# Twenty-two attention projections instead of four made ahead of the first expert block, stored as f32 and finished during the expert blocks

## The chip, the cores and the metric

The program runs on one core of one Trainium2 chip. The metric is the device time of one execution in microseconds (us). The kernel before has a median of 1081.95 us over three runs, which lie between 1077.45 and 1082.16 us.

## What is computed

Input x is (4, 1024, 256): 4 sequences ("batches") of 1024 tokens. The reference, cut to what matters:

```python
xn = layernorm(x)
# attention: 8 query heads of 128, one shared key/value head
q = (xn @ Wq + bq), split into 8 heads;  k, v = split(xn @ Wkv + bkv)
q, k = q + pe, k + pe                     # sinusoidal positions
attn = softmax(causal(q @ k.T / sqrt(128))) @ v
s = concat(attn) @ Wo
# mixture of experts: 8 experts, top 2 per token, hidden size 1024
g = silu(sum over top-2 of gate * (relu(xn @ w1[e] + b1[e]) @ w2[e] + b2[e]))
out = x + s * g
```

A "projection" below is one K, Q or V piece: 512 tokens of one batch against 128 columns of a weight, so K, V and each head's Q have two pieces (j = 0, 1) each. Values are kept as pairs of f16 (high and low part), and a product is three f16 matmul passes (`PASSES`), so a K or Q projection is 6 matmuls of 128x512 and a V projection 24 of 128x128.

## The kernel before, in words

Every engine has its own instruction list, written by hand; engines meet through semaphores. There are three stages, one after the other on TensorE.

**Routing (`routing`).** The rows are normalised and turned into `xT`/`xTb_next`; TensorE makes the router's logits (`logits`), then `project(r)` for four projections of batch 0 (K and the first head's Q), `counts()`, and `place(s)` eight times, which waits for VectorE's one-hot tables (`one_hots`) and yields the list of rows for each expert block. ScalarE scales the first two experts' weights (`weights(q)`), VectorE makes their low halves (`first_low(q)`), GpSimd gathers the rows (`gather`), SyncE's queue writes them to DRAM (`keep`) or turns them (`straight`).

**Expert blocks (`experts`).** 40 blocks; block n multiplies up (L933) while block n-1 multiplies down (L942). The first 22 are of 256 rows, then wide (256) and narrow (128) blocks alternate, then the list ends narrow. ScalarE does the relu of a block in four pairs (L1008), then issues in its own list the turned loads of block n+3 (`load`, L218) and the store of y of block n-2 (`store`, L996). VectorE splits the relu into high and low (`split`, L1032 and L1034) and writes y of block n-2 (`rows`, L1044). GpSimd meanwhile alternates `gather(n)` with `split(p)` of the later experts' weights (L261, L263, L265); SyncE alternates `keep(n)` with `stage(p)`, the load of the raw weights into `wstage`. In four of the last ten blocks one of the stored projections is loaded (L919), gets its positions (L1061), is rounded (L1014) and its low half made (L1065).

**Attention (`attention`).** 32 heads (n = 8 x batch + head), each in five groups of score rows (i = 0 to 4, k = 5n + i). TensorE: `scores` (L1242, L1245), `values` of the head before (L1265, L1267), one projection of the table `Jobs` where it has one for k (L1201), and from head 9 on one `o_tile` of 24 matmuls (L1281). VectorE: row maxima (L1426), low half of the probabilities (L1462), and for a projection `job_positions` (L1435) and `job_low` (L1449, for V L1444). ScalarE: exponentials (L1346), high half (L1376), `job_high` (L1366, for V L1361), and one tanh (L1395) per head. SyncE turns the probabilities by DMA (L1571, `b_pT<-b_ph`). `Jobs` puts the two Q pieces of head n+2 at i = 0 and 2 of head n; the K and V pieces of the next batch at i = 1 of heads 4 to 7 of each batch but the last, in a score bank ("S"); and in head 0 and 1 also V of batch 0.

Of the kernel before, what the change touches and what calls it, by code (L numbers as in the profile page):

```python
# [23 lines left out]
C_ID, C_MASK, C_UP, C_E = 0, P, 2 * P, 3 * P  # L24

# [44 lines left out]
def build(nc, x, wq, bq, wkv, bkv, wo, rw, rb, w1, b1, w2, b2, cst, pe, out):  # L70
# [32 lines left out]
    xT_d = nc.dram_tensor("xn_turned", (NB_ - 1, P, QT * 2 * DC * P), F16, kind="Internal").ap()  # L103
    kq_d = nc.dram_tensor("first_kq", (P, 4, 512), F32, kind="Internal").ap()
    wo_d = nc.dram_tensor("wo_split", (P, 2, HEADS, D), F16, kind="Internal").ap()

    def tensors(ctx):
# [31 lines left out]
    kq_t = Arena(nc, moe.at).take("kq_t", [P, 512], F32)  # L139
# [9 lines left out]
    half = Arena(nc, x_at + NT * D * 2)  # L149
    w_raw.append(half.take("a_w_raw1", [P, PIECES, 512], F32))  # L150
    assert half.at <= raw_end
    xTb_next = top.take("xTb_next", [P, QT, 2 * DC, P], F16)
    wq_late = top.take("wq_late", [P, 2 * DC * HEADS * HD], F16)
# [14 lines left out]
    pe_, kqs_, kql_, kqt_, kqa_, kqb_ = (whole.enter_context(nc.semaphore(s)) for s in (  # L168
        "positions_in", "kq_stored", "kq_loaded", "kq_positions", "kq_hi", "kq_lo"))
# [134 lines left out]
class Jobs:  # L304


    def __init__(self, heads):
        self.at, self.order, self.bank = {}, [], []
        for k in range(5 * heads):
            n, i = k // 5, k % 5  # L310
            b = n // HEADS
            job, bank = None, "J"
            if n == 0:
                job = (("Q", 1, 0), ("Q", 1, 1), ("V", 0, 0), ("V", 0, 1), ("Q", 2, 0))[i]
                bank = ("J", "O0", "O1", "J", "O0")[i]
            elif n == 1 and i < 3:
                job, bank = ("Q", 2 + (i + 1) // 2, (i + 1) % 2), "JSJ"[i]
            elif i in (0, 2) and n + 2 < heads:
                job = ("Q", n + 2, i // 2)
            elif i == 1 and n % HEADS >= 4 and HEADS * (b + 1) < heads:  # L320
                job, bank = ("KKVV"[n % HEADS - 4], b + 1, n % 2), "S"
            if job:
                self.at[k] = len(self.order)
                self.order.append(job)
                self.bank.append(bank)
# [4 lines left out]

    def turned(self, q):

        return sum(1 for p in range(q + 1) if self.order[p][0] != "V")
# [10 lines left out]
def routing(v, ctx, sem, psU):  # L344
# [5 lines left out]
    kq_d, kqs_, wq, wkv, wkv_p, pe_ = (v[k] for k in ("kq_d", "kqs_", "wq", "wkv", "wkv_p", "pe_"))  # L350
# [21 lines left out]
    assert dead.at <= v["x_at"] + NT * D * 2  # L372
    spent = Arena(v["nc"], area.at - (NT - QT) * 2 * DC * P * 2 - NT * 2 * D * 2)
    kq_f = spent.take("a_kq_f", [P, 4, 512], F32)
# [41 lines left out]
    turn_bank, psX, psJ = flat[:4], flat[4], flat[5]  # L416
    psL = psX[:, 0:NT * E]
# [12 lines left out]
    s_kw, s_ks, s_kp, s_kc = map(sem, ("kq_weights_in", "kq_weights_split", "kq_projected", "kq_copied"))  # L430
# [23 lines left out]
    def on_tensor(eng):  # L454
# [27 lines left out]
        def project(r):  # L482

            eng.wait_ge(s_ks, 6)
            j, k = r % 2, 0
            for a, b in PASSES:
                for c in range(DC):
                    w = wkv_p[:, a, c, 0:HD] if r < 2 else wq_p[:, a, c, :]
                    mm = eng.matmul(flat[r].rearrange("p (t n) -> p t n", n=P), w, xTb_next[:, 4 * j:4 * j + 4, 2 * b + c, :],
                                    start=(k == 0), stop=(k == 3 * DC - 1))  # L490
                    k += 1
            mm.then_inc(s_kp, 1)
# [37 lines left out]
        for r in range(3):  # L530
# [3 lines left out]
        project(3)  # L534
        for s in range(CHUNKS):
            place(s)
        eng.wait_ge(s_kc, 4)

    def on_scalar(eng):
# [17 lines left out]
        def weights(q):  # L557
            eng.wait_ge(s_w[q // 4], 16)
            eng.activation(halves(q)[0], v["raw_of"](q), ACT.Copy, scale=WS).then_inc(wh0_, 1)

# [35 lines left out]
        for q in range(PIECES):  # L596
            weights(q)
        eng.wait_ge(s_diff, 1)
        eng.activation(ex[:, 0, :], ex[:, 2, :], ACT.Exp).then_inc(s_e, 1)
        for q in range(PIECES, 2 * PIECES):  # L600
# [1034 lines left out]
```

## Time and profile before

| | |
|---|---|
| three timed runs, median | 1081.95 us |
| lowest and highest | 1077.45, 1082.16 us |
| profiled execution, span of its instructions | 1078.8 us |
| mean granted TensorE clock | 0.984 |
| TensorE (PE) busy | 990.9 us, 92% |
| VectorE (DVE) busy | 857.8 us, 80% |
| ScalarE (ACT) busy | 641.9 us, 59% |
| GpSimd (POOL) busy | 336.8 us, 31% |

The page gives no time of the profiled execution apart from its span, 3.15 us below the median and within the three runs. "Busy" is the time in which an engine had an instruction running. In the trace, a time in us counts from the span's start; "[x <-ENGINE tile]" behind a row is how long the engine was idle before it and what ended that. Expert blocks fill 85 to 471 us, attention the rest.

### The profile page before, as it was taken

To read this page: it belongs to the slowest core of one execution; us is meant where nothing else is said; L and a number is where in the kernel's file an instruction comes from. 1 tells how busy PE (TensorE), PEld (TensorE's weight loads), DVE (VectorE), ACT (ScalarE), POOL (GpSimd) and SP (SyncE) were. 2 spreads that over 40 slices of the span, in tenths; PEclk is the share of its full clock that TensorE was granted. 3 is DMA by queue.
4 is the path that set the end of the run, shared out by engine and by line. 5 is a ranking of instruction groups with operands and counts; after the bars stand their busy time and mean duration, and the time that the engine had idled before them with its cause. 6 is when DMAs were issued, how large, how long until landed. Compare 5 with 4: busy or idle time off the path is not lost.

```text
span 1078.8 us, 25081 instructions
## 1 busy us (share of the span) xinstructions
PE 990.9 (92%) x8686; PEld 778.5 (72%) x8686; DVE 857.8 (80%) x1535; ACT 641.9 (59%) x1358; POOL 336.8 (31%) x350
## 2 busy tenths in 40 slices
PE   0747999999999999998989889999999999999997
PEld 0536888888888898865656667767777677677776
DVE  6985776666766455569999999998999999999971
ACT  2722333233333333357888888878888878788860
POOL 3215999989995000020101002121212111112111
PEclk9968999999999999999999999999999999999999
DMA  8778666666666322149887879798999878888992
GB/s 273 211 287 182 157 181 177 174 179 184 171 172 147 95 60 65 46 121 159 171 154 141 157 142 186 152 164 150 172 189 178 150 150 162 153 171 160 181 179 95
DMA packets 410137, 172.58 MB, mean 160 GB/s; under 512 B 351994, under 2 KB 399940, under 8 KB 409252
## 3 DMA queue, kind: packets, MB, share of 16 engines
q1 hardware_dynamic: 352816, 129.80, 57.5%
q10 hardware_dynamic: 50724, 23.50, 8.6%
q0 software_dynamic: 6480, 17.70, 6.5%
q8 instruction: 77, 1.26, 0.5%
q14 instruction: 40, 0.33, 0.1%
HBM read 52.84 MB, written 31.72 MB: 78 GB/s over the span
## 4 chain that ended last, share of the span: by engine, by line
PE 37%; DVE 10%; DMA 5%; ACT 2%; issue 1%; SPq 0%; ACTq 0%; DVEq 0%
PE b_psO L1265 11%; PE b_psS L1242 11%; PE b_psJ L1281 5%; DMA b_pT<-b_ph 5%; PE b_psJ L1201 5%; DVE b_nmax L1426 3%; DVE b_ph L1462 3%; PE b_psS L1292 2%; PE b_psO L1267 1%; PE b_psS L1201 1%; DVE b_outs L1468 1%; ACT b_pr L1346 1%; ACT b_ph L1376 1%; PE b_psS L1245 1%; DVE b_Q L1449 1%
## 5 line engine op out<-in xcount | busy, mean ns | idle before, releaser
L933 PE MATMUL psU<-bxT,w_p 128*128 128x256 f16 (+1 forms) x1920 | 287.5, 262 | 13.3 <-DVE w_p L276 9.3
L1008 ACT ACTIVATE h<-psU,bias 128x256 f32<-128x256 f32 (+1 forms) x320 | 125.3, 448 | 273.6 <-PE psU L933 171.5
L942 PE MATMUL psY<-w_p,hp 128*128 x1704 | 273.4, 273 | 2.1 <-DVE hp L1034 2.1
L1242 PE MATMUL b_psS<-b_kp,b_Q 128*128 128x512 f16 (+3 forms) x1152 | 218.8, 326 | 1.5 <-PEq L1086 1.5
L1346 ACT ACTIVATE b_pr<-b_psS,b_nmax 128x1024 f32<-128x1024 f32 (+7 forms) x256 | 187.0, 735 | 47.9 <-DVE b_nmax L1426 27.1
L933 PEld LDWEIGHTS psU<-bxT,w_p 128*128 x1920 | 188.4, 98 | 34.0 <-issue 15.1
L1265 PE MATMUL b_psO<-b_pT,b_vp 128*128 128x256 f16 x1536 | 189.7, 274 | 20.3 <-issue 13.5
L1462 DVE SCALAR_TENSOR_TENSOR b_ph<-b_pr,b_rrec,b_ph 128x1024 f16<-128x1024 f32 (+7 forms) x256 | 199.4, 810 | 0.0
L1376 ACT ACTIVATE b_ph<-b_pr,b_rrec 128x1024 f16<-128x1024 f32 (+7 forms) x256 | 187.0, 768 | 15.4 <-DVE b_rrec L1455 14.1
L1032 DVE CAST hp<-h 128x512 f16<-128x512 f32 (+1 forms) x160 | 88.9, 556 | 133.7 <-ACT h L1008 127.5
L1426 DVE TENSOR_REDUCE b_nmax<-b_psS 128x1 f32<-128x1024 f32 (+7 forms) x256 | 183.1, 746 | 13.9 <-PE b_psS L1245 12.4
L942 PEld LDWEIGHTS psY<-w_p,hp 128*128 128x128 f16 x1704 | 166.1, 98 | 23.4 <-issue 3.5
L1265 PEld LDWEIGHTS b_psO<-b_pT,b_vp 128*128 128x128 f16 x1536 | 145.0, 98 | 44.1 <-issue 19.1
L1242 PEld LDWEIGHTS b_psS<-b_kp,b_Q 128*128 128x128 f16 x1152 | 103.2, 98 | 78.9 <-issue 2.2
L1539 POOL DMA_INDIRECT b_yg<-expert_outputs,pos x64 | 68.4, 1069 | 246.1 <-DMA expert_outputs<-y 119.5
L1545 POOL TENSOR_TENSOR b_x_row<-b_G,b_x_row 128x256 f32<-128x256 f32 x24 | 17.4, 727 | 368.6 <-DVE b_G L1489 359.8
L1034 DVE TENSOR_TENSOR hp<-h,hp 128x512 f16<-128x512 f32 (+1 forms) x160 | 127.1, 794 | 5.5
L179 POOL DMA_INDIRECT rowx<-xn_split,who x71 | 78.0, 1099 | 65.9 <-DVE who L796 43.4
L1281 PE MATMUL b_psJ<-b_wo,b_outs 128*128 128x256 f16 x576 | 66.9, 273 | 0.0
L265 POOL TENSOR_TENSOR w_p<-wstage,w_p 128x512 f16<-128x512 f32 x48 | 64.5, 1343 | 4.1
L1366 ACT ACTIVATE b_Q<-b_psJ,bias 128x512 f16<-128x512 f32 x59 | 40.6, 687 | 32.5 <-DVE b_psJ L1435 32.1
L1281 PEld LDWEIGHTS b_psJ<-b_wo,b_outs 128*128 128x128 f16 x576 | 55.2, 98 | 6.5
(187 smaller groups left out, 1027.1 us busy)
## 6 DMA issues: line engine op xcount, KB each, us to landing
wstage<-in_L_ffn_w SPq DMA_DIRECT2D x48, 256.0 KB
expert_rows<-rowx SPq DMA_DIRECT2D x67, 128.0 KB
expert_outputs<-y ACTq DMA_DIRECT2D x31, 256.0 KB
a_x_all<-in_L_attn_x SPq DMA_DIRECT2D x8, 512.0 KB, 9.7
a_w_raw<-in_L_ffn_w SPq DMA_DIRECT2D x4, 1024.0 KB, 9.4
xn_split<-a_xp SPq DMA_DIRECT2D x4, 1024.0 KB, 8.9
xn_turned<-a_xT SPq DMA_DIRECT2D x3, 1024.0 KB, 13.7
b_x_row<-in_L_attn_x SPq DMA_DIRECT2D x24, 128.0 KB, 2.5
```

The costliest lines, as they stand in the source:

```text
L933: mm = eng.matmul(psU[w % U][:, g % 2, 0:tiles * P].rearrange("p (t r) -> p t r", t=tiles), weight(n, a * W1 + c * H + g * P, P), bxT[n % ...
L942: mm = eng.matmul(psY[n % 2][:, t, :], hp[n % 2][:, a, g, t * P:(t + 1) * P], weight(n, 2 * W1 + (2 * g + b) * D, D), start=(g == 0 and k ...
L1008: a = eng.activation(h32[w % 4][:, g, 0:rows], psU[w % U][:, g, 0:rows], ACT.Relu, bias=bias[:, ds(e * HT + 2 * q + g, 1)], scale=1.0 / WS)
L1032: eng.tensor_copy(hi, full).then_inc(hh_, 1)
L1034: eng.tensor_tensor(lo, full, hi, ALU.subtract).then_inc(hl_, 1)
L1242: mm = eng.matmul(dst, Q[n % 3][:, a, u * P:(u + 1) * P], kb[:, c, lo:lo + w], start=(kk == 0), stop=(kk == 2 and not last))
L1265: eng.matmul(both, vb[:, a, j, :], pT[:, at:at + hop + 1:hop, :], start=(j == 0 and kk == 0), stop=False)
L1281: mm = eng.matmul(psJ[:, 0:D], outs[b % many][:, a, h, t * P:(t + 1) * P], wo_p[:, e, h, :], start=(h == 0 and kk == 0), stop=(h == HEADS ...
L1346: a = eng.activation(pr[k % 3][:, o:o + w], psS[BUF[i]][:, :, :].rearrange("p a n -> p (a n)")[:, o:o + w], ACT.Exp, bias=nmax[:, at:at + ...
L1376: a = eng.activation(ph[k % 4][:, 2 * o:2 * o + w], pr[k % 3][:, o:o + w], ACT.Copy, scale=rrec[:, at:at + 1])
L1426: a = eng.tensor_reduce(nmax[:, at:at + 1], psS[BUF[i]][:, :, :].rearrange("p a n -> p (a n)")[:, o:o + w], AX.X, ALU.max, negate=True)
L1462: a = eng.scalar_tensor_tensor(ph[k % 4][:, 2 * o + w:2 * o + 2 * w], pr[k % 3][:, o:o + w], rrec[:, at:at + 1], ph[k % 4][:, 2 * o:2 * o ...
```

## The change

A table `FRONT` names 22 projections: K, Q (head 0) and V of batch 0; K and V of batches 1, 2 and 3; Q of heads 8 and 16. Routing makes all of them, from `xTb_next` and `xT`, in six banks in turn (a seventh waits until the first is copied); ScalarE copies each to f32 in SBUF (`copied`), with the weights of expert 1 scaled in between. `gates()` moves behind `first_low` of expert 0. The raw weights of expert 1 go where `xp` was, so their load now waits for `xn_split`. `xTb_next` is written to DRAM too, by a store that waits in SyncE's list for all 22 copies and stands ahead of `keep(4)`; the load of `b2b` then waits until all turned rows have landed. SyncE stores the f32 results, 512 KB at a time, between `keep(n)` and `stage(p)` (11 times).

One projection is finished per wide block from block 6 on (22 blocks): ScalarE loads it (`kq_load`) behind block n-1, VectorE adds positions (not for V), ScalarE rounds it (`kq_high`), VectorE makes the low half in block n+1, and ScalarE stores both halves (`kq_store`). The first `kq_load` waits for all eleven f32 stores. At the end SyncE loads K and Q of head 0 and `xTb_next` back. In attention SyncE loads V of batch 0 at the start, the next batch's K in head 3 and V in head 4 of each batch, and Q of heads 8 and 16 two heads ahead. `Jobs` keeps only Q pieces.

```diff
+FRONT = tuple([(kind, 0, j) for kind in "KQV" for j in (0, 1)] + [(kind, b, j) for b in (1, 2, 3) for kind in "KV" for j in (0, 1)]
+              + [("Q", m, j) for m in (HEADS, 2 * HEADS) for j in (0, 1)])
...
-            if n == 0:
-                job = (("Q", 1, 0), ("Q", 1, 1), ("V", 0, 0), ("V", 0, 1), ("Q", 2, 0))[i]
-                bank = ("J", "O0", "O1", "J", "O0")[i]
-            elif n == 1 and i < 3:
-                job, bank = ("Q", 2 + (i + 1) // 2, (i + 1) % 2), "JSJ"[i]
-            elif i in (0, 2) and n + 2 < heads:
+            if n == 0 and i < 4:
+                job, bank = ("Q", 1 + i // 2, i % 2), ("J", "O0", "O1", "J")[i]
+            elif n and i in (0, 2) and n + 2 < heads and n + 2 not in FRONT_Q:
                 job = ("Q", n + 2, i // 2)
-            elif i == 1 and n % HEADS >= 4 and HEADS * (b + 1) < heads:
-                job, bank = ("KKVV"[n % HEADS - 4], b + 1, n % 2), "S"
...
+        def copied(r):
+            eng.wait_ge(s_kp, r + 1)
+            eng.activation(kq_f[r // 8][:, r % 8, :], job_bank[(r + 2) % 6], ACT.Copy,
+                           scale=1.0 / WS if FRONT[r][0] == "V" else SC / WS).then_inc(kqc_, 1)
...
+    wide = [n for n in range(6, NBLK) if v["ORDER"][n] < TWIN]
+    KQ_AT = {n: r for r, n in enumerate(wide[:JOBS])}
...
+        eng.wait_ge(kqc_, JOBS)
+        eng.dma_start(v["xT_d"][0], v["xTb_next"][:, :, :, :].rearrange("p t h n -> p (t h n)")).then_inc(xk_, 16)
         for n in range(4, AHEAD):
             v["keep"](eng, n)
+        eng.wait_ge(xk_, 64)
...
+            if n - AHEAD - 4 < JOBS // 2:
+                job_store(n - AHEAD - 4)
...
+        def kq_load(r):
+            if r == 0:
+                eng.wait_ge(kqs_[0], 8 * (JOBS - 16))
+                eng.wait_ge(kqs_[1], 8 * 16)
+                eng.wait_ge(xk_, 64)
+            if r >= 2:
+                eng.wait_ge(kqb_, r - 1)
+            eng.dma_start(kq_t[r % 2][:, :], kq_d[:, r, :]).then_inc(kql_[r % 2], 16)
...
+            if n + 1 in KQ_AT:
+                kq_load(KQ_AT[n + 1])
+            if n - 1 in KQ_AT:
+                kq_store(KQ_AT[n - 1])
             if n >= 2:
                 store(n - 2)
```

TensorE before, from the last logits to the first expert block (`a_oh_r` and `a_oh_q` are the one-hot tables of `place`):

```order
L476 MATMUL psU<-a_rw_p,a_xT 128x8 x48
L489 MATMUL psU<-xTb_next,wkv_p 128x512 x12
L489 MATMUL psU<-xTb_next,a_wq_p 128x512 x6
L499 MATMUL psU<-a_one_100,a_M_109 128x128 x2
L504 MATMUL psU<-a_tri_92,a_tot_93 128x264 x2
L505 MATMUL psU<-a_M_109,a_up_99 128x256
L489 MATMUL psU<-xTb_next,a_wq_p 128x512 x6
L511 MATMUL psU<-a_oh_q,a_oh_r 128x71 x64
L885 TENSOR_LOAD blk_e
```

The same place after, without five of the eight `place` steps:

```order
L508 MATMUL psU<-xTb_next,wkv_p 128x512 x12
L508 MATMUL psY<-xTb_next,a_wq_p 128x512 x12
L519 MATMUL psU<-a_one_105,a_M_114 128x128 x2
...
L499 MATMUL psY<-wkv_p,a_xT 128x128 x48
L531 MATMUL psU<-a_oh_q,a_oh_r 128x71 x8
L508 MATMUL psU<-a_xT,wkv_p 128x512 x3
...
L499 MATMUL psU<-wkv_p,a_xT 128x128 x12
L508 MATMUL psY<-a_xT,wkv_p 128x512 x12
L499 MATMUL psU<-wkv_p,a_xT 128x128 x48
L508 MATMUL psU<-a_xT,a_wq_p 128x512 x12
L508 MATMUL psY<-a_xT,a_wq_p 128x512 x12
L934 TENSOR_LOAD blk_e
```

One whole projection more stands ahead of `counts`, six stand between it and the first `place`, half a one stands behind each `place`, and eight behind the last.

ScalarE after, behind the last relu of block 5 and up to the first relu of block 7 (the four `ISA` and six of the eight relus of block 6 left out); before, the rows of lines L1067 and L1077 are absent here:

```order
L226 DMA_TRANSPOSE bxT_69<-expert_rows 128x4x128 [waits x_kept1]
L1067 DMA kq_t_78<-projected 128x512 [waits xT_kept,projected_stored,projected_stored_late]
L1058 DMA expert_outputs<-y_71 128x2x256 [waits e_rows]
...
L1093 ACTIVATE h_3_137<-psU,bias 128x256
L1077 ACTIVATE kq_h_80<-kq_t_78,bias 128x512 [waits kq_positions]
L226 DMA_TRANSPOSE bxT_67<-expert_rows 128x4x128 [waits x_kept2,e_up]
L226 DMA_TRANSPOSE bxT_67<-expert_rows 128x4x128 [waits x_kept3]
L1067 DMA kq_t_79<-projected 128x512
L1058 DMA expert_outputs<-y_72 128x2x256 [waits e_rows]
```

The load of the first projection, with its wait for every f32 store, now stands ahead of the relus of block 6 on ScalarE.

## Rows read from the trace of the kernel before

**Rows 1.** The page: busy tenths of TensorE in 40 slices of 27 us.
```profile
PE   0747999999999999998989889999999999999997
```
**Rows 2.** Windows: busy us (instructions) of each engine, clock, DMA share, GB/s.
```profile
63.00:76.00 13.00, 10.08 (x64) 7.76 (x64) 11.37 (x26) 3.83 (x8) 0.00 (x0) 0.50 0.75 314
76.00:85.00 9.00, 0.00 (x0) 0.00 (x0) 8.83 (x21) 0.00 (x0) 5.79 (x6) 0.50 0.38 100
...
150.00:330.00 180.00, 180.00 (x1660) 161.45 (x1659) 121.35 (x156) 57.57 (x138) 161.80 (x169) 1.00 0.65 177
```
**Rows 3.** Windows again, in attention, cut at the tanh of heads (L1395).
```profile
521.13:538.25 17.12, 15.18 (x119) 10.36 (x118) 16.23 (x30) 14.64 (x32) 1.89 (x2) 1.00 0.88 170
538.25:610.01 71.76, 64.63 (x524) 44.70 (x523) 68.86 (x123) 60.71 (x127) 7.58 (x8) 1.00 0.81 149
663.21:680.62 17.41, 17.41 (x142) 12.60 (x140) 16.68 (x31) 14.86 (x32) 2.98 (x3) 1.00 0.94 183
680.62:756.93 76.31, 76.31 (x628) 54.68 (x625) 70.29 (x127) 61.81 (x127) 11.78 (x12) 1.00 0.85 154
826.21:902.74 76.53, 76.19 (x627) 54.70 (x625) 70.29 (x127) 61.81 (x126) 11.78 (x12) 1.00 0.84 153
```
**Rows 4.** Timeline of PE, routing to first expert block: start us, us, instructions.
```profile
47.97 4.06 PE L489 MATMUL psU<-xTb_next,wkv_p 128*128 128x512 f16 x12
...
55.42 1.46 PE L489 MATMUL psU<-xTb_next,a_wq_p 128*128 128x512 f16 x6
...
64.35 1.26 PE L511 MATMUL psU<-a_oh_q,a_oh_r 128*128 128x71 f16 x8 [7.47 <-DVE a_oh_q L758]
...
85.12 7.55 PE L933 MATMUL psU<-bxT,w_p 128*128 128x256 f16 x54 [9.34 <-DVE w_p L276]
92.51 0.82 PE L942 MATMUL psY<-w_p,hp 128*128 x6
```
**Rows 5.** Timeline of ACT, ahead of the relus of block 1.
```profile
103.32 1.20 ACT L1008 ACTIVATE h<-psU,bias 128x256 f32<-128x256 f32 x3 [8.17 <-DMA expert_rows<-rowx]
```
**Rows 6.** Timelines of SP and ACT behind the last relu of block 5.
```profile
148.91 0.33 SPq L184 DMA_DIRECT2D expert_rows<-rowx  x1
...
148.73 0.47 ACT L1008 ACTIVATE h<-psU,bias 128x256 f32<-128x256 f32 x1
...
151.13 0.60 ACTq L996 DMA_DIRECT2D expert_outputs<-y  x1
152.47 0.84 ACT L1008 ACTIVATE h<-psU,bias 128x256 f32<-128x256 f32 x2 [3.28 <-issue]
```
**Rows 7.** Landing times of a 256 KB load, and of the 1 MB f32 store.
```profile
DMA to landing us min/median/max: 2.9/3.0/3.6
...
first_kq<-a_kq_f ACTq DMA_DIRECT2D x1, 1024.0 KB, 8.2
```
**Rows 8.** Groups by line on DVE, 150 to 330 and 350 to 440 us, then its timeline.
```profile
L1034 DVE TENSOR_TENSOR hp<-h,hp 128x512 f16<-128x512 f32 x70 | 67.3, 961 | 2.4
...
L1061 DVE TENSOR_TENSOR kq_t<-kq_t,pe_sb 128x512 f32<-128x512 f32 x3 | 2.1, 684 | 0.0
...
144.05 1.53 DVE L1034 TENSOR_TENSOR hp<-h,hp 128x512 f16<-128x512 f32 x1
...
150.41 1.02 DVE L1034 TENSOR_TENSOR hp<-h,hp 128x512 f16<-128x512 f32 x1
...
440.98 0.69 DVE L1034 TENSOR_TENSOR hp<-h,hp 128x512 f16<-128x512 f32 x1
```
**Rows 9.** A group by line and form in attention, 640 to 850 us.
```profile
L1449 DVE SCALAR_TENSOR_TENSOR b_Q<-b_psJ,bias,b_Q 128x512 f16<-128x512 f32 x23 | 17.1, 742 | 0.0
```
**Rows 10.** The chain that ended last, heads 0 to 2: start us, us.
```profile
483.11 0.60 DVE b_vp L1444
...
493.83 1.29 PE b_psS L1201 x6
...
516.84 5.62 DMA b_pT<-b_ph
```

## What the change does to the time, predicted

> **What bounds the kernel now.** I read the page first for where TensorE is full, then windows by stage, then the timelines at the places that the change touches. In the slices TensorE is at 8 or 9 tenths nearly everywhere; after the loads of the input the low ones are the third and fourth, at the end of routing [rows 1]. The windows say what that gap is: from 76 to 85 us TensorE executes nothing, from 63 to 76 us only the 64 short `place` matmuls, and its granted clock is 0.50, the 1.2 GHz level, after the 7.47 us without work before the first `place` [rows 2, 4]. The reader is to see there that VectorE is busy for 11.37 of 13 us and 8.83 of 9 us: routing ends with VectorE, and TensorE waits for it. In the expert blocks it is the reverse: 180.00 us busy of 180, VectorE 121.35, ScalarE 57.57 [rows 2]. In attention there are two regimes [rows 3]. From head 9 on TensorE is busy in all of a head's 17.41 us, and the four heads that carry K and V jobs take 76.31 and 76.53 us. In the first heads TensorE has 2 us of holes in 17.12 and VectorE is busy 16.23; the chain that ended last runs there through VectorE and the turned probabilities (5.62 us for one transfer) [rows 3, 10]. So a projection taken out of attention is worth its TensorE time from head 9 on, and less than that before. A projection put into routing is free as far as it lies under VectorE's work.
>
> **Attention: what is taken out.** Eighteen projections leave (12 of K and V, 2 V of batch 0, 4 Q). Cutting at the tanh of each head:
> - Heads 12 to 15 and 20 to 23: they take 76.31 + 76.53 us and would take 8 x 17.41 = 139.28 without a K or V job, as head 11 does [rows 3]: 13.6 us. Their VectorE work falls to that of head 11 too (16.68 busy), so it does not become the bound.
> - Heads 4 to 7: 71.76 us against 4 x 17.12 [rows 3]: 3.3 us. Less, since VectorE bounds them.
> - Q of heads 8 and 16 leaves heads 6 and 14 with no projection at all. On TensorE one is 1.29 us on the chain [rows 10], so head 14 drops by up to 2.6. VectorE allows it: a Q job takes it some 0.69 us for the positions (the 128x512 addition L1061 is 0.684 [rows 8]) and 0.742 for the low half [rows 9], so its 16.68 us fall to 13.8. I take 2.3. Head 6 is bound by VectorE and ScalarE in turns (14.64 busy), and could give between 0 and 2.9; I take 2.0.
> - V of batch 0 in head 0: two times 0.60 us of VectorE on the chain, and one projection of 1.29 us in head 1 [rows 10]: 2.5 us, bounds 1.2 and 3.
>
> Sum 23.7 us.
>
> **Attention: what is put in.** Eighteen loads of 256 KB on SyncE's list, between the turns of probabilities: two of V at the start, twelve of K and V in heads 3, 4, 11, 12, 19 and 20, four of Q. A 256 KB load lands in 2.9 to 3.6 us [rows 7] and DMA is at 0.8 to 0.9 share there [rows 3]. Those of K, V and Q are wanted two or more heads later, so the loads themselves are hidden; what they can do is make a turn late. From head 9 on TensorE has work queued, and in the first heads a late turn is on the chain [rows 10]. At most four such turns by about 1 us; I take 1.0, bounds 0 and 4.
>
> **Routing.** One projection more is ahead of `counts`. The first twelve matmuls took 4.06 us, the last six 1.46 (1.3 without the drain) [rows 4]; `counts` starts some 0.4 us later. Six projections (8 us) fill the hole up to 64.35 us, half a one (0.65 us) stands beside each `place`, whose pace is VectorE's (eight in the 13 us window [rows 2]). As TensorE then works almost without a break I take the clock to stay at 2.4 GHz, so the last `place` is done at about 75.2 instead of 75.8. Behind it stand 8.5 projections, 8.5 x 1.3 = 11.1 us: the first expert block starts at 86.4, not 85.12 [rows 4]. But before, that block begins at half clock: 7.55 us for its first 54 matmuls, and at 92.51 it is done [rows 4]. At full clock its 48 matmuls take 5.2 us (1660 matmuls in 180.00 us are 0.108 each [rows 2]), which ends at 91.6. So the front is even; I take +0.5 us, bounds -1 and +12 (if the clock stays at half, 8.5 projections take 22 us).
>
> SyncE now waits in front of `keep(4)` for all 22 copies, to about 87, then stores 1 MB, and `b2b` waits until that has landed. The nearest rows: 1 MB lands in 8.2 us when the engines are full [rows 7], and ScalarE already stands 8.17 us for stored rows before the relus of block 1 [rows 5], which TensorE mostly rides out. Later by 1 us of TensorE; bounds 0 and 5.
>
> **Expert blocks: the first load.** `kq_load(0)` stands in ScalarE's list behind block 5, ahead of the relus of block 6, and waits for all eleven f32 stores. The last of these is issued behind `keep(22)`, which is issued at 148.91 us now; ScalarE comes to the load at about 151.1, where its y store stands [rows 6]. 512 KB land in 3 to 5 us (from 3.0 for 256 KB and 8.2 for 1 MB [rows 7]), so at 153 to 154. Eleven stores on the same queue as `wstage` add 5.6 MB to a 43 us stretch, and GpSimd, at 90% busy with no room [rows 2], can fall behind by a few us: 155 to 158. What is queued behind: the y store, then all relus of block 6, then VectorE's halves, and TensorE needs the first of these when it starts block 7, 10.5 us after block 6, the last one four us on. Counting back (0.84 us relus, four times 1.6 us for a split on VectorE, of which L1034 is 0.961 [rows 8], one y row, one addition), a load released by about 155 costs nothing and each us after it costs one. I take 2 us; bounds 0 and 10.
>
> **Expert blocks: the rest.** 22 blocks get two VectorE instructions (one for V) of 0.684 and about 0.742 us [rows 8, 9], one ScalarE activation and two DMA issues. ScalarE is idle 3.28 us for its issues behind a block already [rows 6]; with 1.5 us more, the next block's first relu is 1.5 us late. VectorE has 121 of 180 us of work [rows 2], so it has the time on average: 7 us of 10.5 per block, to become 8.4. It is the phase that can fail: a block's last half has to be ready about 4 us after its last relu and in block 5 the last one is ready 2.2 us after it now (149.20 to 151.43 us) [rows 6, 8]. I take 1.5 us in all for 22 blocks; bounds 0 and 44, from the rivals below.
>
> **Sum.** -23.7 + 1.0 + 0.5 + 1.0 + 2.0 + 1.5 = -17.7 us. On the profiled span of 1078.8 that is 1061.1; on the median, 3.15 us above it, 1064.
>
> **Rivals.**
> - *Shared port, the other side.* VectorE's subtraction L1034 takes 0.961 us on the mean while GpSimd is 90% busy, up to 1.53 us in a single case, and 0.69 us where GpSimd is idle [rows 2, 8]. The addition L1061 was measured only where GpSimd is idle. Nearest to the new instructions is L1034, which also has both operands in SBUF. If both new ones take 1.53 us, a block gets 3.1 us of VectorE and a start 1.5 us later, 4.6 us, against a slack of some 2: 2.6 us lost in each of the 16 blocks in which GpSimd works, 42 us, and the time is 1064 - 1.5 + 42 = 1104. It decides (slower than before) from 1.2 us lost per block. Against it: the mean of L1034 is 0.96, not 1.5, with which the loss is 0 to 0.5 us per block. The Trainium skill, "SBUF — State Buffer", section "SBUF: two separate sides", has it that VectorE and GpSimd share one pair of SBUF ports under an exclusive lock held for a whole instruction, also for a VectorE instruction with two SBUF inputs, which speaks against finishing projections here; by that rule each new instruction could wait out a GpSimd one. The 0.961 against 0.69 us agree with it in direction, far from the full wait.
> - *ScalarE's first load late.* The stores slow `stage`, GpSimd falls behind by 8 to 12 us until unit 22, and TensorE stands 6 to 10 us in block 7: 1070 to 1074, with some lag in the blocks as well. For it: the stores raise DMA share from about 0.65 [rows 2] to over 0.9 (eleven stores of 1.3 to 2 us of all engines in 43 us). Against: `wstage` has two buffers, so a load has about a whole unit of GpSimd's work, over 4 us, until its use, and 256 KB land in 3.0 [rows 7].
> - *The clock stays low in routing*, or the projections are slower there (the first twelve matmuls took 4.06 us, not the 2.6 of two projections at 1.29, for no reason that I read in the trace [rows 4, 10]): block 0 starts 8 to 12 us later, 1074. Against: the fourth projection, at 55.42 us, ran six matmuls in 1.46 us [rows 4].
> - *Nothing is lost*: all costs hidden, 1058 and below.
>
> **How the numbers follow.** As forecast (1058.5 to 1069): 0.55, predicted time 1064. Nothing lost (1054 to 1058.5): 0.10. First load late with lag (1069 to 1078): 0.20. Low clock or slow projections (1070 to 1079): 0.07. Shared port at a price that cancels the gain or more: 0.08. About 0.5%, 5.4 us, is what a measurement of this kernel can tell from no change, so faster means under 1076.5. Faster: 0.55 + 0.10 + 0.17 + 0.04 = 0.86; within 0.5%: 0.03 + 0.03 + 0.02 = 0.08; slower 0.06. The range 1056 to 1076 leaves out some 0.03 below and 0.14 above.
>
> **What the new profile would show.** Clock at 1.00 from 60 to 85 us and the first expert matmul at 86 to 87. Eight heads (12 to 15, 20 to 23) at 17.4 us each, heads 4, 5 and 7 at 17.1, heads 6 and 14 near 15. A wait of ScalarE ahead of the relus of block 6 and, if the step is right, less than 3 us idle of TensorE in block 7. L1034's mean in 150 to 330 us about 1.0. The prediction is wrong if TensorE has idle time in each block from 7 on, if block 0 starts after 90, or if heads 12 to 15 stay above 17.6.

## The result, and the profile after

The changed kernel takes 1101.6 us (median of 4 runs, 1091.8 to 1107.0) beside 1079.7 us of the kernel before on the same chip: the ratio is 1.0208, 95% interval 1.0167 to 1.0249. It is slower by 22 us, where 16 us less were predicted. The trace is of the slowest of the four runs. The profiled execution of after has a span of 1105.0 us.

The page's row of TensorE answers to [rows 1]; the low slices at the end of routing are filled, and the seventh (166 to 193 us) has fallen to 6:

```profile
PE   0798996999999899999898889999999999999997
```

The windows of after, with columns as in [rows 2]: routing, the front of the expert blocks, the stretch of [rows 2], then attention cut as in [rows 3] (head 3, heads 4 to 7, head 6 alone, heads 12 to 15, 20 to 23):

```profile
63.00:77.20 14.20, 13.41 (x118) 11.91 (x116) 10.97 (x24) 5.50 (x10) 0.00 (x0) 1.00 0.58 237
110.00:150.00 40.00, 40.00 (x346) 34.88 (x344) 20.66 (x30) 11.40 (x28) 32.45 (x35) 0.94 0.89 249
150.00:330.00 180.00, 164.10 (x1444) 140.24 (x1443) 132.28 (x154) 55.99 (x133) 157.94 (x161) 0.97 0.79 213
...
564.01:581.12 17.11, 14.94 (x118) 10.25 (x117) 16.23 (x30) 14.64 (x33) 1.89 (x2) 1.00 0.88 170
581.12:649.93 68.81, 57.76 (x449) 40.19 (x448) 62.78 (x113) 57.65 (x120) 7.55 (x8) 0.98 0.92 178
615.33:632.76 17.43, 14.41 (x108) 10.05 (x107) 14.56 (x27) 13.60 (x31) 1.89 (x2) 0.90 0.80 151
...
719.13:788.96 69.83, 68.19 (x558) 49.79 (x557) 64.55 (x117) 58.21 (x120) 12.32 (x12) 1.00 1.00 191
859.23:929.41 70.18, 69.83 (x563) 50.40 (x560) 66.87 (x121) 59.44 (x122) 12.11 (x12) 1.00 0.97 182
```

The kernel before, in the window that [rows 2] did not show:

```profile
110.00:150.00 40.00, 39.73 (x364) 35.36 (x363) 30.18 (x37) 12.66 (x30) 36.75 (x39) 1.00 0.59 162
```

Attention gave 16.0 us of the 22.7 that were forecast. The loss is in the expert blocks: in 150 to 330 us TensorE executed 1444 matmuls, not 1660. Between 110 and 150 us DMA share is 0.89, not 0.59, and GpSimd does 35 instructions instead of 39.

Taking the time of each block's y row on VectorE in both traces, the lag of after grows so: 3.2 us at block 0, 4.4 at block 3, 18.8 at block 4, 30.1 at block 16, 41.7 at block 32, 42.2 at block 39. The y row of block n is made while VectorE splits block n + 2. The jump of 14.3 us at block 4 is the first load. Timelines of PE, DVE and ACT in after, start us, us:

```profile
89.37 3.46 PE L993 MATMUL psU<-bxT,w_p 128*128 128x256 f16 x30 [0.84 <-DMA bxT<-rowx]
...
174.60 1.46 PE L993 MATMUL psU<-bxT,w_p 128*128 128x256 f16 x6 [10.08 <-issue]
```
```profile
173.72 0.68 DVE L1131 SCALAR_TENSOR_TENSOR y<-psY,b2b 128x512 f32<-128x512 f32 x1
```
```profile
155.08 1.70 ACTq L226 DMA_TRANSPOSE bxT<-expert_rows  x1
167.91 0.35 ACTq L1067 DMA_DIRECT2D kq_t<-projected  x1
168.30 0.44 ACTq L1058 DMA_DIRECT2D expert_outputs<-y  x1
169.48 3.02 ACT L1093 ACTIVATE h<-psU,bias 128x256 f32<-128x256 f32 x8 [15.13 <-issue]
```

The trace names no releaser for TensorE's wait of 10.08 us; the y row ends at 174.40, TensorE starts at 174.60, and that y row stands behind the first relus of block 6. ScalarE stands at the load from 156.8 to 167.9 us, since the last f32 store is issued at 164.76 us on SP, behind keep(22), which was issued at 148.91 before [rows 6]. The reader is to see that the wait is SyncE's lateness, and to ask what made SyncE late. SyncE waits for gathers, and those stand in GpSimd's list between its pieces of weights. The first piece that GpSimd finished splitting, before and after:

```profile
106.30 1.21 POOL L265 TENSOR_TENSOR w_p<-wstage,w_p 128x512 f16<-128x512 f32 x1
```
```profile
111.70 0.94 POOL L187 DMA_INDIRECT rowx<-xn_split,who  x1 [9.31 <-DMA expert_rows<-rowx]
...
114.07 1.16 POOL L273 TENSOR_TENSOR w_p<-wstage,w_p 128x512 f16<-128x512 f32 x1
...
130.59 0.94 POOL L269 TENSOR_SCALAR wstage<-wstage 128x512 f32<-128x512 f32 x1 [1.18 <-DMA wstage<-in_L_ffn_w]
```

GpSimd's first piece is 7.8 us late. The wait of 9.31 us alone does not make that, since the kernel before has one of 7.83 us at the same place; the first gather starts 1.6 us later, and the gathers wait 6.4 us in all for the turned rows (`bxT<-rowx`), where they waited 1.1. From there on GpSimd waits for its own loads, which it never does in this stretch before. In after from 105 to 180 us, its waits (in total, times, longest):

```profile
POOL rowx L187 <- DMA expert_rows<-rowx: 9.3, 1, 9.3
POOL wstage L269 <- DMA wstage<-in_L_ffn_w: 7.3, 7, 2.2
```

### The profile page after: what moved, and what is told of

It is laid out like the page before. It is cut to its first block, busy times and chain, and to the rows that moved or that the text cites. A ratio compares the mean times of both kernels' runs of the same rounds, so it can differ in the third digit from the quotient of the medians.

```text
span 1105.0 us, 25182 instructions
## 1 busy us (share of the span) xinstructions
PE 1003.6 (91%) x8686; PEld 782.0 (71%) x8686; DVE 866.8 (78%) x1535; ACT 649.5 (59%) x1376; POOL 342.0 (31%) x350
## 3 DMA queue, kind: packets, MB, share of 16 engines
q10 hardware_dynamic: 56916, 33.98, 12.9%
## 4 chain that ended last, share of the span: by engine, by line
PE 31%; DVE 13%; DMA 4%; ACT 3%; issue 2%; SPq 0%; POOL 0%; ACTq 0%; DVEq 0%
PE b_psS L1333 9%; PE b_psO L1358 9%; DMA b_pT<-b_ph 4%; DVE b_ph L1540 4%; PE b_psJ L1374 4%; DVE b_nmax L1511 4%; PE b_psJ L1297 4%; PE b_psS L1385 2%; DVE b_outs L1546 1%; ACT b_pr L1437 1%; PE b_psO L1360 1%; DVE b_psJ L1519 1%; ACT b_ph L1461 1%; DVE b_Q L1527 1%; PE b_psS L1336 1%
## 5 line engine op out<-in xcount | busy, mean ns | idle before, releaser
L993 PE MATMUL psU<-bxT,w_p 128*128 128x256 f16 (+1 forms) x1920 | 293.6, 264 | 31.1 <-issue 17.2
L1093 ACT ACTIVATE h<-psU,bias 128x256 f32<-128x256 f32 (+1 forms) x320 | 122.1, 450 | 284.6 <-PE psU L993 198.9
L1002 PE MATMUL psY<-w_p,hp 128*128 x1704 | 280.1, 277 | 1.1 <-DVE hp L1121 0.7
L1358 PE MATMUL b_psO<-b_pT,b_vp 128*128 128x256 f16 x1536 | 190.1, 274 | 22.6 <-issue 14.7
L1461 ACT ACTIVATE b_ph<-b_pr,b_rrec 128x1024 f16<-128x1024 f32 (+7 forms) x256 | 187.1, 768 | 18.1 <-DVE b_rrec L1533 16.1
L1623 POOL TENSOR_TENSOR b_x_row<-b_G,b_x_row 128x256 f32<-128x256 f32 x24 | 17.4, 725 | 354.5 <-DVE b_G L1567 345.0
L1546 DVE SCALAR_TENSOR_TENSOR b_outs<-b_psO,bias,b_outs 128x512 f16<-128x512 f32 x64 | 47.2, 738 | 16.5 <-ACT b_outs L1445 16.5
```

The costliest lines, as they stand in the source:

```text
L993: mm = eng.matmul(psU[w % U][:, g % 2, 0:tiles * P].rearrange("p (t r) -> p t r", t=tiles), weight(n, a * W1 + c * H + g * P, P), bxT[n % ...
L1002: mm = eng.matmul(psY[n % 2][:, t, :], hp[n % 2][:, a, g, t * P:(t + 1) * P], weight(n, 2 * W1 + (2 * g + b) * D, D), start=(g == 0 and k ...
L1093: a = eng.activation(h32[w % 4][:, g, 0:rows], psU[w % U][:, g, 0:rows], ACT.Relu, bias=bias[:, ds(e * HT + 2 * q + g, 1)], scale=1.0 / WS)
L1358: eng.matmul(both, vb[:, a, j, :], pT[:, at:at + hop + 1:hop, :], start=(j == 0 and kk == 0), stop=False)
L1461: a = eng.activation(ph[k % 4][:, 2 * o:2 * o + w], pr[k % 3][:, o:o + w], ACT.Copy, scale=rrec[:, at:at + 1])
```

## The experiments

The theory at the outset was that the first load's wait and the finishing in each block make the loss. The rivals were the transfers, the shared port, and GpSimd's weights. e1 to e4, e5 to e8, e9 to e11 and e12 to e14 each have their own runs of the kernel before (medians 1077.9, 1076.5, 1078.2 and 1079.0 us). A time is the median of its runs; traces and lags are of one execution each, which took up to 6.8 us more than that median (e6).

**e1: each load waits for its own store.**
```diff
-            eng.dma_start(kq_d[:, r:r + 2, :], v["job_rows"](r, 2)).then_inc(kqs_[r < 16], 16)
+            eng.dma_start(kq_d[:, r:r + 2, :], v["job_rows"](r, 2)).then_inc(kqs_[r // 2], 16)
...
+            if r % 2 == 0:
+                eng.wait_ge(kqs_[r // 2], 16)
             if r == 0:
-                eng.wait_ge(kqs_[0], 8 * (JOBS - 16))
-                eng.wait_ge(kqs_[1], 8 * 16)
```


> Each finished projection's load waits for its own f32 store alone (eleven semaphores, not two), so ScalarE's load ahead of the relus of block 6 no longer waits until the store behind keep(22) has landed. Theory A (of the 22 us that the change costs, plus the 16 that attention gave, some 14 us are this one wait): no idle stretch of 10 us of TensorE in block 7, 1101.6 - 12 = about 1089 us (1086 to 1093), ratio to the kernel before 1.006 to 1.012. Rival B (the DMA queues are full, and the same transfers make something else late by as much): above 1097. Rival C (GpSimd is behind anyway, and TensorE meets that lag a few blocks later): 1094 to 1100, with a new wait of TensorE for GpSimd's weights.

Measured: 1101.2 us, ratio 1.019 (1.0127 to 1.0253). The wait at the load is gone, and nothing was won by it. TensorE waits elsewhere:

```profile
186.84 1.46 PE L993 MATMUL psU<-bxT,w_p 128*128 128x256 f16 x6 [3.25 <-POOL w_p L273]
...
294.46 1.46 PE L993 MATMUL psU<-bxT,w_p 128*128 128x256 f16 x6 [8.05 <-POOL w_p L273]
```

Rival C, then, with a time 1.2 us above its range: the wait had stood in front of another one. The piece awaited at 186.84 us is the 16th of GpSimd's 56 and the one at 294.46 us the 40th; TensorE needs them at the start of blocks 9 and 18, so the lag shows in the y rows of blocks 7 and 16. From here on the question is GpSimd's pace.

**e2: e1, and the store of xT behind keep(11), so that keeps and b2b don't wait for it.** The line `dma_start(v["xT_d"][0], ...)` moves down, and the waits of SyncE and GpSimd become `xk_` 48 and `kqc_` 22.

> As e1, and the 1 MB store of xT goes out behind keep(8) to keep(11) in place of ahead of keep(4), so neither the keeps nor b2b nor the first split inputs wait for the 22nd projection. Theory A: the 4 to 5 us by which the y rows of blocks 0 to 3 are late come from this wait, so 3 us less than e1 (1 to 4). Rival: they come from the copies and projections in routing and from the full DMA queues (the wait for expert_rows at 109 us), so no more than 1 us below e1.

Measured: 1100.9 us, 1.0182 (1.0122 to 1.0241), the rival's number but not its reason. The y rows of blocks 0 to 3 are on time in this trace (lag below 1 us, 1.2 to 3.5 in e1), yet TensorE waits twice for `w_p`, 10.0 us in all, where it was 11.3 in e1. That this order of the stores brings the first rows on time is not shown either: in e8, which has it too, they are 6.7 to 7.3 us late.

**e3: e1 without VectorE's two instructions per projection.** L1149, L1154 and L1156 are left out (low halves are set to zero once).

> As e1, and VectorE's two instructions per finished projection are left out (positions and low halves are missing from K, Q and V; transfers and ScalarE's part stay). Theory A1 (the 1 us lost in each of 22 blocks is VectorE's time, 0.7 to 1.6 us per instruction beside GpSimd): 15 to 20 us below e1. Rival A2 (it is ScalarE: a load and a store issue and one activation ahead of the next relus): within 5 us of e1. Rival B (the transfers): within 3 us of e1.

Measured: 1096.8 us, 1.0122 (1.0045 to 1.0199), 4 us below e1, with intervals that overlap. From 340 to 440 us TensorE's waits for a y row in e1 and in e3 are almost the same (in total, times, longest):

```profile
PE psU L993 <- DVE y L1131: 6.5, 4, 2.0
```
```profile
PE psU L993 <- DVE y L1132: 5.6, 4, 2.4
```

So most of it isn't VectorE's time: behind block 16 the y rows lose 9.6 us in e3 and 13.6 in e1. That the y row is late because the relus ahead of it are is argued here, and tested by e8.

**e4: e1 without any finishing** (no load, high half, low half or store in the blocks; K, Q and V are filled from xT at the end).

> As e1, but no projection is finished in the expert blocks: no load, no high half, no VectorE part, no store there (K, Q and V then come from xT, 22 stores of it at the end of SyncE's list). The eleven f32 stores, the projections in routing and all of attention's loads stay. Theory A: all that is lost per block is gone, and what stays is the gain of 16 us in attention less 4 to 6 us at the front: 1079.7 - 11 = about 1069 (1065 to 1073). Rival B (the eleven f32 stores and attention's loads cost by themselves): 1075 or above.

Measured: 1083.2 us, 1.0043 (1.0009 to 1.0078), 18 us below e1 and the rival's number. All that is lost after block 17 is gone (a lag of 16.3 us there and 16.3 at block 39), but two waits for `w_p` of 6.75 and 6.40 us stay.

**e5: the kernel before with eleven stores more.**
```diff
+        eng.wait_ge(v["kqs_"], 16)
         for n in range(AHEAD + 4, UNITS):
             v["keep"](eng, n)
+            g = n - AHEAD - 4
+            if g < 11:
+                eng.dma_start(v["more_d"][:, 2 * g:2 * g + 2, :], ...xTb_next[:, 0:4]...).then_inc(v["more_"], 16)
```


> The kernel before, with one thing added: eleven stores of 512 KB (halves of xTb_next into a DRAM area that nobody reads) at the places in SyncE's list where the changed kernel has its f32 stores, behind keep(12) to keep(22). No projection is moved. Theory G (the full DMA queues make GpSimd's weights late, at a pace that has no room, and TensorE meets the lag as one or two waits for w_p): GpSimd waits 7 to 13 us for wstage between 105 and 155 us, TensorE 6 to 12 us for w_p or its like, 1079.7 + 9 = about 1088 (1085 to 1092). Rival (the stores are hidden, what costs is the rest of the change): within 2 us of the kernel before.

Measured: 1090.3 us, 1.0123 (1.0084 to 1.0162): 13.8 us for eleven stores. Waits of GpSimd for its loads from 60 to 180 us, and the one long wait of TensorE:

```profile
POOL wstage L263 <- DMA wstage<-in_L_ffn_w: 9.0, 9, 3.0
```
```profile
284.85 1.46 PE L940 MATMUL psU<-bxT,w_p 128*128 128x256 f16 x6 [8.83 <-POOL w_p L267]
```

The cost comes 130 us after its cause. TensorE was ready at 284.85 - 8.83 = 276.0 us, with a lag of 1.7 us from its earlier blocks (y row of block 15; that of block 16 is 11.0 us late). In the kernel before that piece, the 40th of GpSimd's 56, is done at 270.5 us:

```profile
269.27 1.21 POOL L265 TENSOR_TENSOR w_p<-wstage,w_p 128x512 f16<-128x512 f32 x1
```

So the kernel before had 276.0 - 1.7 - 270.5 = 3.9 us of room there, and GpSimd, busy 161.8 of 180 us [rows 2], has little means to make up a delay before that: e5's lag at the 20th piece, 12.0 us, is 14.3 at the 40th.

**e6: e4 without the f32 stores as well** (the copied projections go nowhere).

> As e4 (no finishing in the expert blocks) and the eleven f32 stores are left out too, so the copied projections go nowhere. Theory G: TensorE's two waits for w_p (6.7 and 6.4 us in e4) shrink to 0 to 5 us, and the time is 1083.2 - 11 = about 1072 (1068 to 1076). If GpSimd's later start alone (first w_p 5 us later) decides: 1078 or more. Rival (the stores have nothing to do with it): 1083.

Measured: 1072.5 us, 0.9967 (0.9942 to 0.9991). GpSimd has no wait for its loads of experts' weights up to 180 us and 2.7 us of them behind that, and TensorE waits once for `w_p`, 2.9 us. Its first piece is 9.4 us late and its 40th 12.9, against 5.0 and 19.4 in e4.

**e7: e1 with the stores in 22 pieces of 256 KB, one behind each keep.**

> As e1, the f32 stores in 22 pieces of 256 KB, one behind each keep from 12 to 33, not eleven of 512 KB behind keeps 12 to 22; same bytes, at half the rate. Theory G: GpSimd loses 2 to 5 us between its first and twelfth unit, not 10, TensorE's waits for w_p fall from 11 us to under 6, 1101 - 7 = about 1094 (1090 to 1097). Rival (bytes count and not when they go): 1099 or above.

Measured: 1102.3 us, 1.0222 (1.0176 to 1.0267): the rival. The 12th piece is late by 11.7 us, not 13.8, but by the 26th it is 20.4 (17.4 in e1). The stores now run beside the loads and stores of the finishing, which may be why; no run separates the two.

**e8: e2 with the finishing elsewhere in the block.**
```diff
                 a.then_inc(rl_, 1)
+                if q == 0 and n in KQ_AT:
+                    kq_load(KQ_AT[n])
+                if q == 1 and n - 1 in KQ_AT:
+                    kq_high(KQ_AT[n - 1])
+                if q == 2 and n - 2 in KQ_AT:
+                    kq_store(KQ_AT[n - 2])
...
-                if q == 0 and n in KQ_AT and FRONT[KQ_AT[n]][0] != "V":
+                if q == PAIR - 1 and n in KQ_AT and FRONT[KQ_AT[n]][0] != "V":
...
-                if q == 0 and n - 1 in KQ_AT:
+                if q == PAIR - 1 and n - 1 in KQ_AT:
```


> As e2, and the finishing sits elsewhere in a block: ScalarE's load, high half and store between its relu pairs, where it waits for TensorE anyway, and VectorE's two instructions behind its last split. Theory P (the 9 to 16 us that finishing costs in e1 above e4 come from where it stands: ScalarE's 1.5 us ahead of a block's first relus, VectorE's ahead of its second split): 8 to 14 us below e2, 1087 to 1093. Rival Q (the transfers of 22 loads and 22 stores, or the sum of VectorE's time): within 4 us of e2's 1101.

Measured: 1087.6 us, 1.0089 (1.0057 to 1.0122), 13 us below e2: theory P. No wait for a y row is left. The run moves ScalarE's and VectorE's part together; that ScalarE's is the larger one rests on e3 alone. What is left is GpSimd's weights, and at 112 us a wait for rows that GpSimd gathers and SyncE's queue stores (PE's waits from 95 to 515 us):

```profile
PE psU L993 <- POOL w_p L273: 13.6, 2, 8.4
PE psU L993 <- DMA bxT<-expert_rows: 6.6, 1, 6.6
```

**e9: twelve projections ahead, not 22.** `FRONT` is K and Q of batch 0 and K and V of batches 2 and 3; the others are jobs of attention as before. `KQ_AT` takes `wide[12:24]`.

> Twelve projections ahead of the first block, not 22: K and Q of batch 0 as in the kernel before, and K and V of batches 2 and 3, which fill heads 12 to 15 and 20 to 23; the ten others stay in attention as before. f32 stores of 256 KB behind every second keep, xT in four parts behind keeps 21 to 27, finishing in wide blocks 18 to 36 and placed as in e8. Theory G (what counts is how late GpSimd's weights are; before, it has about 2 us of room): GpSimd starts 2 to 5 us late, loses 2 to 4 us to 3 MB of stores, TensorE is 4 to 6 us late at the start of attention, and attention gives 12.8 us at heads 12 to 15 and 20 to 23: 1078 - 8 = about 1070 (1066 to 1074), faster than both kernels. Rival (the start of GpSimd slips as much as with 22 projections, by 8 to 10 us): 1074 to 1077.

Measured: 1075.0 us (12 runs), 0.9967 (0.9948 to 0.9986): 0.3% faster than before, some 3.6 us, which is less than expected. The number lies in the rival's range, but its reason did not come: GpSimd starts 2.3 us late, as theory G had it. It loses 6.3 us more by the 24th piece and 2.3 more by the 40th, not 2 to 4. TensorE's wait for `w_p` is 4.4 us, and it enters attention 8.1 us late.

**e10 and e12: all 22, stores spread and xT late.** Stores of 256 KB leave behind keeps 12 to 40 and xT in four parts among them. e10 finishes in wide blocks from 8 on; e12 is e10 with one line changed, and finishes in blocks 11 to 32:
```diff
-    KQ_AT = {n: r for r, n in enumerate(wide[2:2 + JOBS])}
+    KQ_AT = {n: r for r, n in enumerate(range(11, 11 + JOBS))}
```


> All 22, as e8, with f32 stores of 256 KB (one behind each keep from 12 to 25, then behind every second one), xT stored in four parts behind keeps 27 to 33, and the finishing two wide blocks later. Theory G: GpSimd no longer starts behind 1 MB of xT, so 3 us less lag, and its lag at unit 40 is 18 to 23 us, not 27: 1083 (1079 to 1086), still not faster than the kernel before, since the bytes are the same. Rival (placement alone decides, bytes do not): GpSimd's lag under 12 us and 1073.

> As e10, with the finishing in blocks 11 to 32 (wide and narrow), not in wide blocks from 8 on, so that the first load no longer waits for the last part of xT, stored behind keep(33). Theory G: the wait of 25.5 us of TensorE is gone, GpSimd's lag of 16 us at unit 40 in e10 becomes TensorE's, with attention 15 us shorter: 1078 to 1082. Rival (without that wait GpSimd's units see more transfers again, and its lag is that of e8): 1086 or above.

Measured: e10 1092.2 us, 1.0127 (1.0109 to 1.0145); e12 1083.2 us, 1.0039 (1.0011 to 1.0067). e10, 6 us above its range, has one long wait, behind its first load, which waits for the last part of xT:

```profile
211.95 1.46 PE L1006 MATMUL psY<-w_p,hp 128*128 x6 [25.50 <-DVE hp L1125]
```

Without it GpSimd's 40th piece is 21.1 us late (15.1 in e10, where TensorE stood still for these 25.5 us), and the time lies between the two expectations.

**e11: e8 without attention's sixteen later loads** (K and V zero or old, an older Q in heads 8 and 16).

> As e8, but attention's sixteen loads of finished K, V and Q for the later batches and heads 8 and 16 are left out (K and V are zero in batches 1 and 3, those of batch 0 stay in batch 2, and heads 8 and 16 use an older Q). Theory L (attention gained 15.5 us and not 22.7 because heads 2 to 9 are held by the loop through the one buffer of turned probabilities, and the loads cost little): attention's length within 1.5 us of e8's. Rival (the loads make the turns late): 5 us or more shorter, most of it in heads 10 to 22.

Measured: 1079.1 us in its one run. From the last y row to the last tanh attention takes 557.1 us. The eleven kernels with all loads lie between 559.1 (e12) and 564.6 us (e6), after at 560.6 and e8 at 562.0, with a mean of 561.7. So the loads cost about 4.6 us by that mean, between the theory and the rival; with one run of e11, and the nearest of the eleven 1.9 us above it, the size is rough.

**e13 and e14: GpSimd's scaling left out** of the kernel e8 and of the kernel before (the weights it splits stay 64 times too small).
```diff
-        eng.tensor_scalar(full, full, WS, 1.0, ALU.mult, ALU.mult).then_inc(ws_, 1)
-        eng.wait_ge(ws_, p - FIRST + 1)
```


> As e8, but GpSimd's scaling of each piece of weights by 64 (L269, 0.64 us) is left out, so the experts from the third on, Wq and Wo have weights 64 times too small; every transfer stays. Theory G (GpSimd's pace of 4.17 us per unit is the bound): it makes up its lag of 20 us at some 0.7 us per unit, TensorE's waits for w_p fall from 13.6 to under 6 us, 1087.6 - 12 = about 1075 (1069 to 1079). Rival (the DMA queues set the pace, GpSimd would only wait longer for wstage): 1084 or above.

> The kernel before with the same instruction left out of GpSimd's split. TensorE has no wait for w_p there now, so theory G gives the same time as before (within 3 us). Should it be faster by more, GpSimd's instructions also lengthen VectorE's or the block in another way.

Measured: e13 1072.9 us, 0.9946 (0.9919 to 0.9974), 14.7 us below e8 with every transfer kept; e14 1077.3 us, 0.9996 (0.9965 to 1.0027), no change, though GpSimd's 40th piece is 23.7 us early in it. So leaving GpSimd's instruction out wins time where its weights come late and none, within 3 us, where they don't. In e13 GpSimd now does wait for its loads, 22.8 us by 180 us, but catches up after that: its pieces are 18.0 us late at the 20th, 12.2 at the 40th and 6.5 at the 56th, and TensorE has no wait for `w_p`. The wait of GpSimd in e13 from 60 to 180 us:

```profile
POOL w_p L269 <- DMA wstage<-in_L_ffn_w: 22.8, 11, 5.2
```

**One table for all.** Lags against the one trace of the kernel before, in us, read from the timelines of POOL and DVE. If GpSimd decides, the y row of block 16 is late by the lag of the 40th piece less the 3.9 us of room:

| kernel | 1st piece | 40th piece | less 3.9 | y row, block 16 | y row, block 39 |
|---|---|---|---|---|---|
| e6 | 9.4 | 12.9 | 9.0 | 9.1 | 10.7 |
| e9 | 2.3 | 10.9 | 7.0 | 7.9 | 8.1 |
| e5 | 2.0 | 14.3 | 10.4 | 11.0 | 10.5 |
| e4 | 5.0 | 19.4 | 15.5 | 16.1 | 16.3 |
| e12 | 9.3 | 21.1 | 17.2 | 17.7 | 19.3 |
| e1 | 5.4 | 23.9 | 20.0 | 21.4 | 35.0 |
| e8 | 10.2 | 27.5 | 23.6 | 24.2 | 26.3 |
| after | 7.8 | 22.4 | 18.5 | 30.1 | 42.2 |
| e13 | 9.6 | 12.2 | 8.3 | 11.4 | 8.1 |
| e2 | 4.0 | 24.9 | 21.0 | 21.6 | 36.5 |
| e3 | 9.7 | 27.9 | 24.0 | 24.2 | 33.8 |
| e7 | 6.4 | 23.5 | 19.6 | 21.9 | 34.9 |
| e11 | 4.3 | 17.9 | 14.0 | 14.9 | 17.6 |
| e10 | 6.4 | 15.1 | 11.2 | 32.0 | 28.0 |
| e14 | -6.4 | -23.7 | | -4.0 | -7.6 |

Ten kernels follow GpSimd within 1.4 us and e7 within 2.3. In these TensorE does wait for that very piece, so the agreement says that the 3.9 us, taken from e5, hold for all of them; that the lateness is the cause is shown by taking it away, in e6 and e13. The kernel after and e10 lie well above, where the first load had cost more already; e13 lies above because its front alone was 9 us late; and e14 has no lateness. The blocks behind 16 add 12 to 15 us where the finishing stands ahead of the relus (after, e1, e2, e7), 9.6 where VectorE's part of it is left out (e3), and under 3 in the other kernels.

## Why the prediction was wrong

- **Attention, taken out and put in: mechanism right, size off.** Forecast 22.7 us net; from the last y row to the last tanh it is 16.0 us shorter (576.5 to 560.6). Heads 4 to 7 gave 3.0, of 3.3 for K and V and 2.0 for head 6. Heads 12 to 15 gave 6.5 and 20 to 23 6.3, together 12.8, of 13.6 and 2.3 for head 14 (16.32 us, not near 15). Head 6 without a projection takes 17.43 us. TensorE stands 3.02 us in it before 21 matmuls, which then take 4.00 us, at a granted clock of 0.60 between 620.4 and 624.5 us, where the same 21 take 2.45 us in the heads beside it; these 4 us lie on the chain that ended last:

```profile
620.44 4.00 PE L1358 MATMUL b_psO<-b_pT,b_vp 128*128 128x256 f16 x21 [3.02 <-issue]
...
639.09 2.45 PE L1358 MATMUL b_psO<-b_pT,b_vp 128*128 128x256 f16 x21 [3.44 <-DMA b_pT<-b_ph]
```

  So TensorE, with a projection less, stood idle longer there (3.02 us, 2.17 in head 5), and the low clock behind it took 1.55 us. The row of 639.09 shows that such an idle time is not always followed by the low clock, and the kernel before has one slow run of this kind too, in head 8 (3.67 us), which after has not. Why heads 6 and 7 together stay at 34.6 us, where 32.2 were forecast, is otherwise open; VectorE is busy 14.56 of the 17.43 us. The loads cost about 4.6 us (e11), a little over the bound of 4, and not 1.0. The 2.5 us of heads 0 and 1 did not come: the first tanh is 34.4 us behind the last y row, 33.7 before (32.1 to 34.4 in the kernels with all 22).
- **Routing: right in the clock, off in the size.** The granted clock is 1.00 from 63 us on, where it was 0.50 [rows 2]. The first expert matmul is at 89.4 us, not 86.4: the interleaved pairs ran at 1.71 us each, since a `place` holds TensorE 1.04 us at the full clock too and half a projection 0.67, so the last `place` starts at 76.2 and ends 2 us later than forecast. With the later wait for expert rows, block 3 is 4.4 us late; 1.5 were forecast.
- **Expert blocks, the first load: the step that failed first, 2 us against 14.3.** Its rule, a microsecond for each one after 155, was about right: the load was issued at 167.9. Its input was wrong. I let GpSimd "fall behind by a few us", and it fell behind by 8 at the start and 13 by the tenth piece.
- **What the step left out matters more.** GpSimd's lateness was priced only through SyncE's store. But TensorE itself needs GpSimd's weights, with 3.9 us of room at the start of block 18. "GpSimd, at 90% busy with no room" stood in the prediction as a remark and had no term of the sum. Where nothing else holds TensorE, its lag at the end of the expert blocks is 10.7 us without stores or finishing (e6), 16.3 with the stores (e4), 26.3 with the finishing's transfers (e8), with the lag of the front in it (at block 3: 6.2, 0.3 and 7.3 us). This is why e1, which takes the 14 us away, wins nothing.
- **Expert blocks, the rest: 1.5 us forecast, 23 between blocks 4 and 32.** In after TensorE has no wait for `w_p` in this stretch, so this is the finishing. It is not the shared port in the main: without VectorE's instructions most of the loss stays (e3). What is left is ScalarE's load, high half and store ahead of the next relus; with all of the finishing placed where ScalarE and VectorE wait, 13 us of it are gone (e8), and the y rows behind block 16 lose 2.1 us in place of 14.9. The sentence "the next block's first relu is 1.5 us late" named this, and was then set against an average slack that the block's last half does not have.
- **The rivals.** The shared port was given the loss of each block, and its threshold, 1.2 us per block, was about what was lost, for another reason. The new VectorE instructions do take longer beside GpSimd: L1149 1147 ns on the mean between 150 and 330 us, against 684 where GpSimd is idle [rows 8]. The Trainium skill, "SBUF — State Buffer", section "SBUF: two separate sides", has a VectorE instruction with two SBUF inputs and a GpSimd instruction that reads SBUF block each other; the trace agrees in direction, at 0.46 us per instruction, and leaving all of VectorE's part out gave 4 us (e3), not clear of the noise.
- **Open.** Why GpSimd's first piece is 4 to 10 us late among kernels with the same routing (5.4 and 9.7 in e1 and e3, 4.0 and 10.2 in e2 and e8) was not settled. With one trace of each kernel it may differ as much between two executions of one kernel, and it moves each 22-projection kernel by some microseconds. With four and twelve projections in front it is 2.0 (e5) and 2.3 (e9).

## What to carry to other kernels

An engine off the critical path that is busy almost without a break sets a pace of its own: compute for its last product how long before its use it is ready (here 3.9 us), and price every added transfer ahead of it against that number, wherever the cost will show. When a wait is long, ask before removing it what stands behind it: the first one removed here (the first load's) was worth nothing, the second (the finishing's place) 13 us, the third (GpSimd's weights) 15. And work that is put into an engine's idle time belongs at the place in its list where it waits, not ahead of what others wait for.

## What was not expected of the hardware

In e5 eleven stores of 512 KB beside loads of 256 KB made GpSimd 12 us late by its 20th piece and the kernel 13.8 us slower, at a DMA share of 0.87 in place of 0.59 between 110 and 150 us: GpSimd waited 9.0 us for its loads although the share was well below 1. Half the rate of the same stores did not make the kernel faster (e7). In head 6 of after, which has a projection less, 21 matmuls on the chain took 4.00 us and not 2.45, at a granted clock of 0.60, behind 3.02 us of idle time of TensorE. And GpSimd waited 22.8 us for its loads in e13, more than the 11.3 in e8, in a kernel that was 15 us faster: a wait of an engine says little until one knows whether its next product is late.
